# Two cross-attention layers on one core: row-bias sums and weight totals computed in another way, with new orders of the steps

## The chip, the cores and the metric

The kernel runs on one core of a Trainium2 chip. The core has five engines that work at the same time, each strictly in the order of its own instruction stream: TensorE (PE; its weight loads are listed as PEld), VectorE (DVE), ScalarE (ACT), GpSimd (POOL) and SyncE (SP), which here only starts DMAs. They wait for each other through semaphores. SBUF and PSUM are the on-chip memories of 128 partitions; TensorE writes to PSUM. The metric is the device time in microseconds of one execution.

## The reference

For each of 8 batches, `x` is 512 x 256 and `ctx` is 1601 x 128. The first layer's softmax runs over the queries (axis 1), the second's over the context rows. `bq0` and so on are the layer's biases.

```
q = x @ Wq0 + bq0 ; k = ctx @ Wk0 + bk0 ; v = ctx @ Wv0 + bv0
w = softmax(q @ k.T / 16, over the 512 queries)
y = x + w @ v
y = (y - mean) * rsqrt(var + 1e-6) * gamma + beta          # over the 256 features
Q = y @ Wq1 + bq1 ; K = ctx @ Wk1 + bk1 ; V = ctx @ Wv1 + bv1
P = softmax(Q @ K.T / 16, over the 1601 context rows)
out = y + (P @ V) @ Wo + bo
```

## The kernel before

The key projections are folded into the queries: with `A0 = Wq0 @ Wk0.T` the scores of layer 0 are `ctx @ (x A0 + ...).T` plus a term per query, `x @ u0` with `u0 = Wq0 @ bk0`. That term, 512 numbers per batch, is the row bias of layer 0 (`z0`, then `cb`). Layer 1 has the same, `c1`, from the normalised rows `xhat` and `u1_gamma`. As the softmax of layer 0 is over the queries, the weights of one query don't sum to one over the context rows. The value bias `bv0` is therefore multiplied by each query's total weight (`wsum`, then `rowsum0`).

Products that need full precision are made of rounded parts: each operand is split into a high part (ScalarE casts it to float32r) and a low part (the difference, by VectorE where the source is PSUM, by GpSimd where it is SBUF), and `split3` (lines 652 to 656) issues three matmuls.

A batch's 1601 context rows are 13 tiles, 12 of 128 and one of 65. Steps are small functions, named below with (batch, index):

- Layer 0: `turn_ctx` and `turn_x` transpose the inputs on TensorE, `project_q0` makes the folded queries, `project_bias0` spreads `z0` over the partitions, `scores0` makes one tile of scores, `max0` (L1171, VectorE) reads it from PSUM, adds the row bias and takes the extreme, `exp0`, `recip0` and `norm0` make the weights, `p0_high` and `p0_low` (L1383, GpSimd) split them, and `weigh0` accumulates the weighted context. `sum_weights` (L1373, L1376, GpSimd) adds the weights over the tiles into `wsum`, and `sum_rows0` (L748, TensorE) sums that over the partitions, by a matmul with a column of ones.
- Between the layers: `bias_x0` (L1198, L1209, VectorE) adds `rowsum0 * bv0` and `x`, `predict` and `residual0` add the values, `moments0`, `rsqrt_var` (GpSimd) and `normalised` (L1240) give `xhat`, `turn_y` (L768) transposes it and `project_q1` (L774) projects it. `q1_high` (ScalarE) and `q1_low` (L1250, VectorE) split the result.
- Layer 1: `scores1` makes the scores of one block of 128 rows in four chunks, `rowmax1` (L1257) and `bias1_of` (L1268) take the row's maximum and combine it with `c1`, `exp1` (L1048, ScalarE) makes the weights, `turn_p1` (L800) transposes them, `p1_turned` and `p1_low` split them, `weigh1` accumulates, `project_out`, `residual1` (GpSimd) and `finish` (L1290) make the output.

The row biases are made in two steps each. `weigh_u0` (L1407) and `weigh_u1` (L1414) multiply 128 x 1024 elements on GpSimd into the buffer `xr`; `sum_z0` (L1161) and `bias_row1` (L1246) sum them over 256 features on VectorE. `row_bias1` (L1031) then adds a constant on ScalarE. Batch 0's product of layer 0 is made on VectorE (`weigh_u0_first`). A product-and-sum in one instruction exists once, at L1346, for the constant.

Batches are pipelined: while layer 0 works on batch a, layer 1 works on batch b = a - 1, and the first steps of batch c = a + 1 begin. The order of the steps on each engine is written out in tables, one for TensorE, ScalarE, VectorE and GpSimd: a head, a part that is repeated for a = 2 to 5, and a tail. An engine never goes around a step that waits. Loads and stores are issued by SP in a fixed order of their own: the four context groups of a batch, its x, then the store of the batch three before. Each load waits until its buffer is free; the load of x waits for `bias_x0` of the batch two before.

## Time and profile before

| | us |
|---|---|
| median of 3 runs | 467.65 |
| lowest, highest | 466.14, 468.08 |
| profiled execution, first to last instruction (span) | 464.6 |
| TensorE busy | 443.7 (96%) |
| ScalarE busy | 383.7 (83%) |
| VectorE busy | 366.8 (79%) |
| GpSimd busy | 365.0 (79%) |

The profile gives the profiled execution's time as its span alone; the median of the runs lies 3.05 us above it. All times in rows are of that execution, counted from its first instruction. A row's duration reaches from an instruction's start to its end, and the next one on the same engine may start before that end; the distance from start to start is called pitch here. The granted clock of TensorE is 1.00 throughout. TensorE's matmuls overlap a good deal (a 512-column one lasts 0.39 us at a pitch of 0.23), so its cost is read from pitches. In the rows `a<-b,c` is the output and its inputs, `x4` a count, and what stands in square brackets is idle time before the instruction and who ended it.

### The profile page before, as it was taken

Reading aid. Unit: us, or ns where it says so; the run is one execution under the profiler, and the core shown is the slowest. Engines: PE = TensorE matmul, PEld = TensorE weight load, DVE = VectorE, ACT = ScalarE, POOL = GpSimd, SP = SyncE. Lnnn points to the kernel's source line nnn. Section 1 sums busy time; section 2 is a strip of 40 time slices with the busy share of each in tenths; the row PEclk is TensorE's granted clock in tenths of the full one; section 3 lists DMA queues with packets and bytes.
Section 4 is the critical chain, followed back from the end, with each engine's and each line's share of the span. In section 5 each row is a group of like instructions: output and inputs, shape, how many; then the busy total and the mean of one; then the engine's idle time right before and its main releaser. Section 6 shows DMA issues by size and latency. Waiting matters only on the chain.

```text
span 464.6 us, 7967 instructions
## 1 busy us (share of the span) xinstructions
PE 443.7 (96%) x2433; PEld 371.6 (80%) x2433; DVE 366.8 (79%) x898; ACT 383.7 (83%) x819; POOL 365.0 (79%) x321
## 2 busy tenths in 40 slices
PE   8798899999999999999999999999999999799796
PEld 8686667887888888888888878888888878687596
DVE  3798978788886988778787888779877887578774
ACT  4899889987999789987899879987899879872473
...
DMA packets 23896, 17.29 MB, mean 37 GB/s; under 512 B 1055, under 2 KB 23854, under 8 KB 23854
## 3 DMA queue, kind: packets, MB, share of 16 engines
...
## 4 chain that ended last, share of the span: by engine, by line
PE 79%; ACT 8%; DVE 5%; POOL 4%; issue 4%; DVEq 0%; POOLq 0%; ACTq 0%
PE ps_l L654 11%; PE ps_l L655 10%; PE ps_l L656 9%; PE ps_s L800 9%; PE ps_s L654 8%; PE ps_s L656 8%; PE ps_s L655 8%; ACT p L1048 3%; PE ps_s L774 3%; PE ps_s L841 3%; DVE max L1257 2%; POOL wsum L1376 2%; PE ps_l L687 2%; ACT p L1001 2%; PE ps_s L768 2%
## 5 line engine op out<-in xcount | busy, mean ns | idle before, releaser
L1376 POOL TENSOR_TENSOR wsum<-wsum,p 128x512 f32<-128x512 f32 (+1 forms) x88 | 116.3, 1322 | 13.4 <-ACT p L1007 11.8
L1383 POOL TENSOR_TENSOR p_lo<-p,p_hi 128x512 fp32r<-128x512 f32 (+1 forms) x91 | 117.2, 1295 | 2.6 <-ACT p_hi L1015 2.4
L1001 ACT ACTIVATE p<-s_sb,min 128x512 f32<-128x512 f32 (+1 forms) x104 | 75.4, 726 | 7.5 <-DVE min L1171 5.3
L1171 DVE CUSTOM_DVE_ANT_0 s_sb<-ps_l,cb 128x512 f32<-128x512 f32 (+1 forms) x104 | 70.4, 685 | 13.3 <-ACT p L1001 5.5
L1007 ACT ACTIVATE p<-p,r 128x512 f32<-128x512 f32 (+1 forms) x104 | 74.9, 728 | 1.4 <-DVE r L1178 1.3
L1192 DVE TENSOR_TENSOR p1T_lo<-ps_s,p1T_hi 128x512 fp32r<-128x512 f32 (+1 forms) x91 | 60.6, 683 | 14.4 <-ACT p1T_hi L1056 13.9
L1257 DVE TENSOR_REDUCE max<-ps_s 128x1 f32<-128x804 f32 x58 | 57.1, 992 | 10.0 <-PE ps_s L656 8.6
L1056 ACT CAST p1T_hi<-ps_s 128x512 fp32r<-128x512 f32 (+1 forms) x91 | 52.0, 586 | 14.9 <-PE ps_s L800 12.1
L1015 ACT CAST p_hi<-p 128x512 fp32r<-128x512 f32 (+1 forms) x104 | 63.5, 624 | 0.5 <-PE ps_l L656 0.4
L1048 ACT ACTIVATE p<-ps_s,bias 128x1206 f32<-128x1206 f32 (+1 forms) x58 | 53.6, 927 | 3.6 <-DVE bias L1268 3.1
L800 PE MATMUL ps_s<-ident,p 128*128 128x128 f32 (+1 forms) x364 | 49.6, 273 | 1.5 <-ACT p L1048 1.5
L800 PEld LDWEIGHTS ps_s<-ident,p 128*128 128x128 f32 (+1 forms) x364 | 43.2, 141 | 9.3 <-ACT p L1048 1.9
L654 PE MATMUL ps_l<-p_hi,ctx_lo 128*128 128x512 f32 (+1 forms) x104 | 45.5, 437 | 2.4 <-POOL p_lo L1383 2.2
L654 PE MATMUL ps_l<-qw_hi,ctxT_lo 128*128 128x512 f32 (+1 forms) x104 | 46.6, 448 | 0.7 <-DVE min L1171 0.7
L1364 POOL TENSOR_TENSOR ctx_lo<-ctx_sb,ctx_hi 128x512 fp32r<-128x512 f32 (+1 forms) x32 | 35.2, 1101 | 12.4 <-ACT ctx_hi L974 12.4
L654 PE MATMUL ps_s<-p1T_hi,ctx_lo 128*128 128x512 f32 (+2 forms) x104 | 43.9, 422 | 0.8 <-DVE p1T_lo L1280 0.8
L654 PE MATMUL ps_s<-ctxT_hi,qw_lo 128*128 128x402 f32 x116 | 42.2, 364 | 2.2 <-ACT p L1048 2.0
L656 PE MATMUL ps_l<-p_hi,ctx_hi 128*128 128x512 f32 (+1 forms) x104 | 41.0, 394 | 0.0
L655 PE MATMUL ps_l<-qw_lo,ctxT_hi 128*128 128x512 f32 (+1 forms) x104 | 41.0, 394 | 0.0
L656 PE MATMUL ps_l<-qw_hi,ctxT_hi 128*128 128x512 f32 (+1 forms) x104 | 41.0, 394 | 0.0
L655 PE MATMUL ps_l<-p_lo,ctx_hi 128*128 128x512 f32 (+1 forms) x104 | 40.9, 393 | 0.0
L656 PE MATMUL ps_s<-ctxT_hi,qw_hi 128*128 128x402 f32 x116 | 40.0, 345 | 0.0
...
## 6 DMA issues: line engine op xcount, KB each, us to landing
...
```

Source lines behind the costliest of these rows:

```text
L654: nc.tensor.matmul(ps, w_lo, m_hi, start=start, stop=False)
L655: nc.tensor.matmul(ps, w_hi, m_lo, start=False, stop=False)
L656: return nc.tensor.matmul(ps, w_hi, m_hi, start=False, stop=stop)
L800: mm = nc.tensor.transpose(ps_turn[i % 3][0:m, t * P:(t + 1) * P], p1[:, t, i * P:i * P + m], ident[:])
L1001: nc.scalar.activation(p0[0:m, ring0(i), :], s0_sb[0:m, (a + i) % 2, :], ACT.Exp, bias=min0[0:m, i:i + 1], scale=-1.0, accum_out=sum0[0:m, ...
L1007: nc.scalar.activation(p0[0:m, ring0(i), :], p0[0:m, ring0(i), :], ACT.Copy, scale=r0[0:m, i:i + 1]).then_inc(norm0_done, 1)
L1015: nc.scalar.copy(p0_hi[0:m, (MT * a + i) % RH, :], p0[0:m, ring0(i), :]).then_inc(p0_hi_done, 1)
L1048: nc.scalar.activation(exps, scores, ACT.Exp, bias=bias1[:, t:t + 1], scale=1.0, accum_out=sum1[:, h, t:t + 1]).then_inc(exp1_done, 1)
L1171: nc.vector.tensor_tensor_reduce(out=s0_sb[0:m, (a + i) % 2, :], in0=ps_s0[0:m, (a + i) % 2, :], in1=cb[a % 2][0:m, :], scale=-SCALE, scal ...
L1257: nc.vector.tensor_reduce(max1[:, t, k:k + 1], s1_banks(b, t)[:, 2 * k:2 * k + 2, 0:CHUNK], AX_XY, ALU.max).then_inc(max1_done, 1)
L1376: nc.gpsimd.tensor_tensor(total, total, p0[0:m, ring0(i), :], ALU.add).then_inc(wsum_done, 1)
L1383: nc.gpsimd.tensor_tensor(p0_lo[0:m, h, :], p0[0:m, ring0(i), :], p0_hi[0:m, h, :].bitcast(F32), ALU.subtract).then_inc(p0_lo_done, 1)
```

## The change

- `weigh_u0_first`, `weigh_u0`, `sum_z0` and `weigh_u1` are removed. `row_bias0` and the new `bias_row1` make each row bias with four product-and-sum instructions of 128 x 256 on VectorE; their product goes to `xr` and is not used, and layer 1's constant comes in as the start value of the sum. `row_bias1` on ScalarE is removed.
- `sum_rows0` transposes the four blocks of `wsum` into the whole PSUM bank, and `bias_x0` sums over 128 columns each on VectorE.
- The waits are adapted: a group now counts four. `row_bias0` of batch a waits for `bias_row1` of batch a - 2, since both write `xr`; `bias_x0` waits for both as before.
- All four order tables are new. The last part of an iteration now holds layer 1's first steps and `turn_x`, `x_turned` and `xT_low` of batch a + 2 (role "d").

The code parts of the diff, and of the order tables the new repeated parts of VectorE and GpSimd, the end of TensorE's and the beginning of ScalarE's:

```
 TENSOR_STEADY = (
...
+    ("weigh1", "b", 6), ("weigh1", "b", 7), ("turn_p1", "b", 11), ("predict", "a", 0), ("weigh1", "b", 8),
+    ("weigh1", "b", 9), ("predict", "a", 1), ("turn_p1", "b", 12), ("scores0", "c", 5), ("weigh1", "b", 10),
+    ("weigh1", "b", 11), ("weigh1", "b", 12), ("turn_ctx", "c", 2), ("weigh0", "c", 0), ("project_out", "b", 0),
+    ("project_out", "b", 1), ("turn_y", "a", 0), ("turn_y", "a", 1), ("turn_x", "d", 0), ("scores0", "c", 6),
+    ("project_q1", "a", 0), ("weigh0", "c", 1), ("weigh0", "c", 2), ("scores0", "c", 7),
...
 SCALAR_STEADY = (
...
+    ("norm0", "a", 6), ("exp0", "a", 7), ("exp1", "b", 0), ("x_turned", "c", 1), ("norm0", "a", 7), ("exp1", "b", 1),
+    ("exp0", "a", 8), ("p0_high", "a", 6), ("norm0", "a", 8), ("p0_high", "a", 7), ("exp1", "b", 2),
+    ("q0_high", "c", 0), ("exp1", "b", 3), ("exp0", "a", 9), ("p0_high", "a", 8), ("ctx_high", "a", 3),
+    ("norm0", "a", 9), ("exp0", "a", 10), ("exp1", "b", 4), ("p0_high", "a", 9), ("exp1", "b", 5), ("norm0", "a", 10),
...
 VECTOR_STEADY = (
-    ("bias_row1", "b", 0), ("q1_low", "b", 0), ("recip0", "a", 5), ("max0", "a", 6), ("max0", "a", 7),
...
-    ("rowmax1", "b", 3), ("bias1_of", "b", 1), ("max0", "a", 9), ("max0", "a", 10), ("sum_z0", "c", 0),
+    ("recip0", "a", 7), ("max0", "a", 8), ("max0", "a", 9), ("xT_low", "c", 1), ("rowmax1", "b", 2),
+    ("recip0", "a", 8), ("rowmax1", "b", 3), ("bias1_of", "b", 1), ("row_bias0", "c", 0), ("max0", "a", 10),
     ("q0_low", "c", 0), ("rowmax1", "b", 4), ("recip0", "a", 9), ("rowmax1", "b", 5), ("bias1_of", "b", 2),
...
-    ("recip0", "c", 3), ("p1_low", "b", 12), ("residual0", "a", 1), ("moments0", "a", 1), ("normalised", "a", 0),
-    ("normalised", "a", 1), ("max0", "c", 4), ("ctxT_low", "c", 2), ("recip0", "c", 4), ("finish", "b", 0),
-    ("finish", "b", 1), ("max0", "c", 5),
+    ("ctxT_low", "a", 3), ("max0", "a", 11), ("recip0", "a", 10), ("max0", "a", 12), ("rowmax1", "b", 6),
+    ("rowmax1", "b", 7), ("bias1_of", "b", 3), ("ctxT_low", "c", 0), ("recip0", "a", 11), ("max0", "c", 0),
+    ("max0", "c", 1), ("recip0", "a", 12), ("p1_low", "b", 0), ("p1_low", "b", 1), ("recip0", "c", 0),
+    ("p1_low", "b", 2), ("p1_low", "b", 3), ("p1_low", "b", 4), ("max0", "c", 2), ("ctxT_low", "c", 1),
+    ("recip0", "c", 1), ("max0", "c", 3), ("p1_low", "b", 5), ("p1_low", "b", 6), ("p1_low", "b", 7),
+    ("bias_x0", "a", 0), ("recip0", "c", 2), ("p1_low", "b", 8), ("at0_low", "a", 0), ("p1_low", "b", 9),
+    ("p1_low", "b", 10), ("recip1", "b", 0), ("recip0", "c", 3), ("residual0", "a", 0), ("moments0", "a", 0),
+    ("residual0", "a", 1), ("p1_low", "b", 11), ("p1_low", "b", 12), ("moments0", "a", 1), ("normalised", "a", 0),
+    ("max0", "c", 4), ("normalised", "a", 1), ("ctxT_low", "c", 2), ("bias_row1", "a", 0), ("recip0", "c", 4),
+    ("finish", "b", 0), ("finish", "b", 1), ("max0", "c", 5), ("xT_low", "d", 0), ("max0", "c", 6),
+    ("q1_low", "a", 0), ("recip0", "c", 5), ("max0", "c", 7), ("rowmax1", "a", 0), ("recip0", "c", 6),
+    ("rowmax1", "a", 1), ("bias1_of", "a", 0),
 )
...
 GPSIMD_STEADY = (
-    ("rsqrt_var", "b", 0), ("p0_low", "a", 1), ("sum_weights", "a", 2), ("rsqrt_var", "b", 1), ("weigh_u1", "b", 0),
...
-    ("weigh_u0", "c", 0), ("p0_low", "a", 6), ("sum_weights", "a", 7), ("p0_low", "a", 7), ("sum_weights", "a", 8),
...
+    ("p0_low", "a", 3), ("p0_low", "a", 4), ("sum_weights", "a", 4), ("ctx_low", "a", 2), ("p0_low", "a", 5),
+    ("sum_weights", "a", 5), ("sum_weights", "a", 6), ("p0_low", "a", 6), ("p0_low", "a", 7), ("sum_weights", "a", 7),
+    ("p0_low", "a", 8), ("sum_weights", "a", 8), ("sum_weights", "a", 9), ("p0_low", "a", 9), ("p0_low", "a", 10),
+    ("residual1", "b", 0), ("sum_weights", "a", 10), ("sum_weights", "a", 11), ("sum_weights", "a", 12),
+    ("p0_low", "a", 11), ("p0_low", "a", 12), ("ctx_low", "a", 3), ("sum_weights", "c", 1), ("p0_low", "c", 0),
+    ("p0_low", "c", 1), ("rsqrt_var", "a", 0), ("ctx_low", "c", 0), ("p0_low", "c", 2), ("rsqrt_var", "a", 1),
+    ("ctx_low", "c", 1), ("sum_weights", "c", 2), ("sum_weights", "c", 3),
 )
...
@@ -710,7 +699,7 @@
                 mm.then_inc(qw0_ps, 1)
 
             def project_bias0(a, _):
-                pe.wait_ge(z0_done, a + 1)
+                pe.wait_ge(z0_done, TB * (a + 1))
                 misc_free("project_bias0", a)
                 for t in range(TB):
                     mm = nc.tensor.transpose(ps_misc[:, t * P:(t + 1) * P], z0[:, t:t + 1].broadcast_to([P, P]), ident[:])
@@ -745,8 +734,7 @@
                 pe.wait_ge(wsum_done, summed(a, MT - 1))
                 misc_free("sum_rows0", a)
                 for t in range(TB):
-                    mm = nc.tensor.matmul(ps_misc[:, t:t + 1], wsum[a % 2][:, t * P:(t + 1) * P], ones[:, 0:1],
-                                          start=True, stop=True)
+                    mm = nc.tensor.transpose(ps_misc[:, t * P:(t + 1) * P], wsum[a % 2][:, t * P:(t + 1) * P], ident[:])
                 mm.then_inc(rowsum_ps, 1)
 
             def predict(a, h):
@@ -1026,10 +1014,6 @@
                     act.wait_ge(row1_made, MADE)
                 nc.scalar.copy(xhT[:, c, :], ps_y[c]).then_inc(xhT_done, 1)
 
-            def row_bias1(b, _):
-                act.wait_ge(c1_part_done, b + 1)
-                nc.scalar.activation(c1[:], c1_part[:], ACT.Identity, bias=c1_const[:, 0:1], scale=1.0).then_inc(c1_done, 1)
-
             def q1_high(b, _):
                 act.wait_ge(qw1_ps, b + 1)
@@ -1147,18 +1131,18 @@
                 nc.vector.scalar_tensor_tensor(qw0_lo[a % 2][:], ps_misc[:], qb0, qw0_hi[a % 2][:].bitcast(F32),
                                                ALU.add, ALU.subtract).then_inc(qw0_lo_done, 1)
 
-            def weigh_u0_first(a, _):
-
-                dve.wait_ge(u0_done, 1)
-                dve.wait_ge(x_loaded[0], 16)
-                nc.vector.tensor_tensor(xr[:], x_sb[0][:], u0_row[:].unsqueeze(1).broadcast_to([P, TB, E]), ALU.mult
-                                        ).then_inc(xu0_done, 1)
-
-            def sum_z0(a, _):
-                dve.wait_ge(xu0_done, a + 1)
+            def row_bias0(a, _):
+
+                if a == 0:
+                    dve.wait_ge(u0_done, 1)
+                if a >= 2:
+                    dve.wait_ge(c1_done, TB * (a - 1))
                 if a > 0:
                     dve.wait_ge(cb_ps, a)
-                nc.vector.tensor_reduce(z0[:], xr[:], AX_X, ALU.add).then_inc(z0_done, 1)
+                dve.wait_ge(x_loaded[a % 2], 16 * (a // 2 + 1))
+                for t in range(TB):
+                    nc.vector.tensor_tensor_reduce(out=xr[:, t, :], in0=x_sb[a % 2][:, t, :], in1=u0_row[:], scale=1.0, scalar=0.0,
+                                                   op0=ALU.mult, op1=ALU.add, accum_out=z0[:, t:t + 1]).then_inc(z0_done, 1)
 
             def max0(a, i):
 
@@ -1195,14 +1179,15 @@
             def bias_x0(a, _):
 
                 dve.wait_ge(rowsum_ps, a + 1)
-                nc.vector.tensor_copy(rowsum0[:], ps_misc[:, 0:TB]).then_inc(rowsum_done, 1)
+                nc.vector.tensor_reduce(rowsum0[:], ps_misc[:].rearrange("p (t m) -> p t m", m=P), AX_X, ALU.add
+                                        ).then_inc(rowsum_done, 1)
                 if a == 0:
                     dve.wait_ge(rows_loaded, 16 * 2)
                     dve.wait_ge(row1_made, MADE)
                 else:
-                    dve.wait_ge(c1_part_done, a)
+                    dve.wait_ge(c1_done, TB * a)
                 if a < B - 1:
-                    dve.wait_ge(z0_done, a + 2)
+                    dve.wait_ge(z0_done, TB * (a + 2))
                 dve.wait_ge(x_loaded[a % 2], 16 * (a // 2 + 1))
                 dve.wait_ge(rowsum_done, a + 1)
                 for t in range(TB):
@@ -1242,8 +1227,15 @@
 
             def bias_row1(b, _):
 
-                dve.wait_ge(u1_part_done, b + 1)
-                nc.vector.tensor_reduce(c1_part[:], xr[:], AX_X, ALU.add).then_inc(c1_part_done, 1)
+                dve.wait_ge(xhat_done, TB * (b + 1))
+                if b == 0:
+                    dve.wait_ge(row1_made, MADE)
+                else:
+                    dve.wait_ge(bias1_done, TB * b)
+                for t in range(TB):
+                    nc.vector.tensor_tensor_reduce(out=xr[:, t, :], in0=xhat[:, t, :], in1=u1_gamma[:], scale=1.0,
+                                                   scalar=c1_const[:, 0:1], op0=ALU.mult, op1=ALU.add,
+                                                   accum_out=c1[:, t:t + 1]).then_inc(c1_done, 1)
 
             def q1_low(b, _):
                 dve.wait_ge(qw1_hi_done, b + 1)
@@ -1260,7 +1252,7 @@
             def bias1_of(b, t):
 
                 if t == 0:
-                    dve.wait_ge(c1_done, b + 1)
@@ -1397,23 +1389,6 @@
                     ins = nc.gpsimd.tensor_tensor(y_res[:, t, :], y_res[:, t, :], betaob_row[:], ALU.add)
                 ins.then_inc(y_res_done, 1)
 
-            def weigh_u0(a, _):
-
-                pool.wait_ge(x_loaded[a % 2], 16 * (a // 2 + 1))
-                if a == 1:
-                    pool.wait_ge(z0_done, a)
-                else:
-                    pool.wait_ge(c1_part_done, a - 1)
-                nc.gpsimd.tensor_tensor(xr[:], x_sb[a % 2][:], u0_row[:].unsqueeze(1).broadcast_to([P, TB, E]), ALU.mult
-                                        ).then_inc(xu0_done, 1)
-
-            def weigh_u1(b, _):
-
-                pool.wait_ge(xhat_done, TB * (b + 1))
-                pool.wait_ge(row1_made, MADE)
-                nc.gpsimd.tensor_tensor(xr[:], xhat[:], u1_gamma[:].unsqueeze(1).broadcast_to([P, TB, E]), ALU.mult
-                                        ).then_inc(u1_part_done, 1)
-
             def rsqrt_var(a, h):
                 pool.wait_ge(var_done, 2 * a + h + 1)
                 two = slice(2 * h, 2 * h + 2)
```

## Rows read from the trace of the kernel before

**Rows 1.** The page's part 1: busy time, share and instructions of each engine.

```profile
PE 443.7 (96%) x2433; PEld 371.6 (80%) x2433; DVE 366.8 (79%) x898; ACT 383.7 (83%) x819; POOL 365.0 (79%) x321
```

**Rows 2.** Three stretches: us; busy of PE, PEld, DVE, ACT, POOL; clock, DMA.

```profile
50.00:102.00 52.00, 49.15 (x260) 39.42 (x259) 41.93 (x104) 47.26 (x100) 47.83 (x42) 1.00 0.09 28
208.30:261.50 53.20, 52.95 (x289) 44.59 (x288) 43.55 (x107) 46.79 (x100) 47.50 (x42) 1.00 0.12 36
370.00:418.60 48.60, 45.45 (x243) 37.55 (x241) 35.28 (x88) 38.79 (x80) 42.34 (x38) 1.00 0.03 11
```

**Rows 3.** The chain that ended last: start, length in us, what.

```profile
285.22 1.81 DVE max L1257 x2
287.56 1.37 ACT p L1048 x2
```

**Rows 4.** TensorE in order of time: start, length in us; two places.

```profile
202.98 0.95 PE L748 MATMUL ps_l<-ones,wsum 128*128 128x1 f32 x8
203.79 0.47 PE L654 MATMUL ps_l<-p_hi,ctx_lo 128*128 128x512 f32 x1
...
239.90 0.60 PE L716 MATMUL ps_l<-ident,z 128*128 128x128 f32 x4
240.25 0.48 PE L654 MATMUL ps_l<-qw_hi,ctxT_lo 128*65 128x512 f32 x1
```

**Rows 5.** By form: line, engine, op, count; busy us, mean ns; idle before.

```profile
L1414 POOL TENSOR_TENSOR xr<-xhat,u_gamma 128x1024 f32<-128x1024 f32 x8 | 19.0, 2380 | 5.1 <-DVE xhat L1240 5.1
...
L1280 DVE TENSOR_TENSOR p1T_lo<-ps_s,p1T_hi 128x256 fp32r<-128x256 f32 x24 | 9.3, 420 | 4.8 <-ACT p1T_hi L1063 4.0
```

**Rows 6.** VectorE in order of time, around the row sum of layer 0.

```profile
233.87 0.68 DVE L1171 CUSTOM_DVE_ANT_0 s_sb<-ps_l,cb 128x512 f32<-128x512 f32 x1
234.47 0.69 DVE L1171 CUSTOM_DVE_ANT_0 s_sb<-ps_l,cb 128x512 f32<-128x512 f32 x1
235.08 1.21 DVE L1161 TENSOR_REDUCE z<-xr 128x4 f32<-128x1024 f32 x1
236.21 0.74 DVE L1147 SCALAR_TENSOR_TENSOR qw_lo<-ps_l,small,qw_hi 128x512 fp32r<-128x512 f32 x1
```

**Rows 7.** A wait of an operation with two SBUF inputs: VectorE, then GpSimd.

```profile
98.57 0.88 DVE L1209 SCALAR_TENSOR_TENSOR xr<-bv_row,rowsum,x_sb 128x256 f32<-128x256 f32 x1
...
97.86 1.30 POOL L1383 TENSOR_TENSOR p_lo<-p,p_hi 65x512 fp32r<-65x512 f32 x1
```

**Rows 8.** The product-and-sum that is already there: VectorE, then GpSimd.

```profile
38.28 0.79 DVE L1346 CUSTOM_DVE_ANT_0 xhat<-p,scaled 128x256 f32<-128x256 f32 x1
...
36.96 1.82 POOL L1376 TENSOR_TENSOR wsum<-wsum,p 128x512 f32<-128x512 f32 x1
```

**Rows 9.** The operation of rows 7 with GpSimd idle: VectorE.

```profile
258.28 1.67 DVE L1209 SCALAR_TENSOR_TENSOR xr<-bv_row,rowsum,x_sb 128x256 f32<-128x256 f32 x4
```

**Rows 10.** Around the normalised rows: VectorE, then GpSimd, then TensorE.

```profile
216.01 0.73 DVE L1240 TENSOR_SCALAR xhat<-xr,mv,rstd 128x256 f32<-128x256 f32 x2 [0.27 <-POOL rstd L1420]
218.84 1.66 DVE L1290 SCALAR_TENSOR_TENSOR y_res<-ps_s,r,y_res 128x256 f32<-128x256 f32 x4
222.88 0.75 DVE L1250 SCALAR_TENSOR_TENSOR qw_lo<-ps_s,scaled,qw_hi 128x512 fp32r<-128x512 f32 x1 [0.47 <-ACT qw_hi L1035]
...
224.16 3.90 POOL L1383 TENSOR_TENSOR p_lo<-p,p_hi 128x512 fp32r<-128x512 f32 x3
...
217.97 1.04 PE L768 MATMUL ps_s<-ident,xhat 128*128 128x128 f32 x8
220.24 1.88 PE L774 MATMUL ps_s<-xhT,a_gamma 128*128 128x512 f32 x4
224.03 0.35 PE L654 MATMUL ps_s<-ctxT_hi,qw_lo 128*128 128x402 f32 x1
```

**Rows 11.** The place in layer 1's scores: ScalarE, then TensorE.

```profile
239.43 1.27 ACT L1048 ACTIVATE p<-ps_s,bias 128x1206 f32<-128x1206 f32 x1
...
241.03 0.34 PE L654 MATMUL ps_s<-ctxT_hi,qw_lo 128*128 128x402 f32 x1
```

More of the change, by code:

```diff
@@ L287 @@
[L287 removed]
[3 rows of a table removed]
[L291 to L293 removed]
+    ("sum_weights", 0, 11), ("sum_weights", 0, 12), ("sum_weights", 1, 1), ("ctx_low", 1, 0), ("p0_low", 1, 0),
@@ new lines @@
+    ("sum_weights", 6, 11), ("sum_weights", 6, 12), ("p0_low", 6, 11), ("p0_low", 6, 12), ("ctx_low", 6, 3),
+    ("residual1", 5, 0), ("sum_weights", 7, 1), ("p0_low", 7, 0), ("ctx_low", 7, 0), ("rsqrt_var", 6, 0),
+    ("rsqrt_var", 6, 1), ("p0_low", 7, 1), ("p0_low", 7, 2), ("sum_weights", 7, 2), ("p0_low", 7, 3),
+    ("p0_low", 7, 4), ("ctx_low", 7, 1), ("sum_weights", 7, 3), ("sum_weights", 7, 4), ("p0_low", 7, 5),
+    ("sum_weights", 7, 5), ("p0_low", 7, 6), ("p0_low", 7, 7), ("sum_weights", 7, 6), ("sum_weights", 7, 7),
@@ L319 @@
+    ("sum_weights", 7, 8), ("p0_low", 7, 8), ("sum_weights", 7, 9), ("ctx_low", 7, 2), ("p0_low", 7, 9),
+    ("p0_low", 7, 10), ("p0_low", 7, 11), ("sum_weights", 7, 10), ("sum_weights", 7, 11), ("sum_weights", 7, 12),
+    ("p0_low", 7, 12), ("ctx_low", 7, 3), ("residual1", 6, 0), ("rsqrt_var", 7, 0), ("rsqrt_var", 7, 1),
+    ("residual1", 7, 0),
 )
@@ L1350, in _ @@
             steps = {f.__name__: f for f in (
-                ctxT_low, xT_low, at0_low, bias_x0, q0_low, weigh_u0_first, sum_z0, max0, recip0, residual0, moments0, normalised, bias_row1,
+                ctxT_low, xT_low, at0_low, bias_x0, q0_low, row_bias0, max0, recip0, residual0, moments0, normalised, bias_row1,
                 q1_low, rowmax1, bias1_of, recip1, p0_low_first, p1_low, p1_low_half, finish, prepare_w1)}
@@ L1429, in _ @@
             steps = {f.__name__: f for f in (
-                ctx_low, sum_weights, p0_low, rsqrt_var, weigh_u0, weigh_u1, residual1)}
+                ctx_low, sum_weights, p0_low, rsqrt_var, residual1)}
             pre0()
```

58 lines of the change are left out of this document (25 added, 33 removed), and 433 rows, old and new, of tables (GPSIMD_HEAD, GPSIMD_STEADY, SCALAR_HEAD, SCALAR_STEADY).

## The prediction

> **What bounds the kernel now.** I read the shares first [rows 1], then the stages, then the chain of waits, then single places in order of time. The shares say TensorE: 443.7 of 464.6 us, the other three near 80%. The stages say where [rows 2]: in a middle batch (53.20 us long) TensorE is busy 52.95, VectorE 43.55, GpSimd 47.50. It is idle for 2.85 us in the second batch's stretch and for 3.15 in the seventh's; only there does a slack GpSimd have something to give. So in the middle only two things count: TensorE instructions saved, and anything that comes so late that TensorE waits. The second is near, though TensorE looks full: the chain leaves it in every middle batch for two maxima of layer 1's scores on VectorE and two exponentials on ScalarE before TensorE goes on [rows 3]. VectorE has 9.65 us idle per batch, but it works in order, and a delay in front of such a maximum is not spread over them.
>
> **The change part by part.**
>
> *sum_rows0.* Four fp32 matmuls with one column are eight instructions and hold TensorE from 202.98 to 203.79, 0.81 us. Four transposes of 128x128, here those of z, take 239.90 to 240.25, 0.35 us [rows 4]. The saving is 0.46 us per batch, 8 x 0.46 = 3.7 us, all of it on the path in the middle.
>
> *bias_x0.* The copy of 4 columns becomes a sum over 512 columns in PSUM: some 0.6 us by the pitch of a 512-wide operation [rows 6], instead of under 0.1, so 0.5 us more VectorE per batch. It lies beside weigh0 and weigh1 on TensorE; sum_rows0 also moves ahead of the last weigh0 steps. Cost 0; without that cover it would be 0.5 x 8 = 4 us.
>
> *GpSimd's products go.* 2.38 us each [rows 5], two per batch, 4.8 of 47.5 us, so GpSimd falls to 42.7 of 53.2, 80%. In the middle GpSimd is not the bound, so this is worth 0 there. At the two ends it may shorten the waits for p_lo and wsum. The ends are 0 and the whole idle time of the two stretches, 6.0 us [rows 2]. I take half, 3.0. ScalarE's row_bias1 (four columns) goes too: 0.
>
> *VectorE's product-and-sums.* Each group of four replaces one reduction of 1024 columns, which is 1.13 us of VectorE (235.08 to 236.21). Alone, a product-and-sum over 512 columns has a pitch of 0.60 with its accumulator read (233.87 to 234.47) [rows 6]. 256 columns less are 0.27 less (0.69 us for 512 columns [rows 6] against 420 ns for 256 [rows 5]). So one costs 0.33 and a group 1.33, 0.2 us more than now. That is nothing, if nothing else happens.
>
> But these operations read both inputs from SBUF, unlike the maxima in layer 0, whose first input is PSUM. The trace shows what happens to such a one while GpSimd is at work. bias_x0's operation started at 98.57, GpSimd's running one ended at 99.16, and it ended at 99.45 [rows 7]: 0.29 after GpSimd's end, instead of 0.48 after its own start. The product-and-sum that exists already started at 38.28 and ended at 39.07, GpSimd's at 38.78, again 0.29 later [rows 8]. So it waits until GpSimd's whole instruction is over, then needs its own time. With GpSimd idle four such operations take 1.67 us [rows 9]; seven of the eight groups of bias_x0 are like that, because GpSimd happens to be waiting there. The new groups stand elsewhere.
>
> The Trainium skill, "SBUF — State Buffer", section "Who interferes with whom", says that a VectorE instruction with two SBUF inputs and a GpSimd instruction that reads SBUF shut each other out, and that the one issued second waits for the first one's end. The traces agree where they show it (0.29 after GpSimd's end, twice). By that rule a waiting GpSimd instruction also gets in between two of a group's four, which would give the forecast below; without it the sum would be the first rival's.
>
> The waits per group: the first operation meets a running GpSimd instruction four times in five (80% load), on average half over. One lasts 1.25 us by pitch (three in 3.90) [rows 10]: 0.5 us. For the other three no row shows who gets in when VectorE's one ends with GpSimd waiting. The ends are 0 (VectorE keeps its turn) and 3 x 1.25 + 1.25 = 5.0 in all. I take turns one after the other where GpSimd has work ready, since the rows show that neither breaks into the other.
>
> *Site 1, bias_row1.* It stands behind normalised and ctxT_low, ahead of finish, max0, xT_low, max0 and q1_low. GpSimd then has ctx_low, two sum_weights and a p0_low in line, all but the last fed early by ScalarE; with such a line it runs without a gap today [rows 10]. Wait W1 = 0.5 + two more of 1.25 = 3.0. How much is hidden? xhat is done at 216.66 (216.01 and two pitches of 0.33). Then 0.60 + 1.33 + 0.10 + 1.73 + 0.61 + 0.61 + 0.61 brings VectorE to q1_low at 222.25. qw_hi, now there at 222.88, comes 0.37 earlier, since turn_y is followed by a turn of x and one scores0 only (1.90 instead of the 2.27 from 217.97 to 220.24): 222.51. q1_low ends at 223.20; TensorE reaches scores1 at 223.7 (224.03 less 0.37) [rows 10]. Slack 0.26 + 0.50 = 0.76; TensorE waits 3.0 - 0.76 = 2.2 us.
>
> *Site 2, row_bias0.* It stands behind bias1_of of the second row block, ahead of max0, q0_low and the next two maxima, which feed the exponential before the last scores1. Today that exponential ends at 240.70 and scores1 starts at 241.03: slack 0.33 [rows 11]. One max0 (0.61) now comes before the site instead of behind, against 0.2 for the group: slack 0.7. GpSimd has p0_low and sum_weights of tile 7 ready, then waits for p0_high of tile 8, which ScalarE issues behind two exponentials. W2 = 0.5 + 1.25 + 0.8 x 1.25 = 2.7; TensorE waits 2.0 us.
>
> Both sites recur in 6 batches with layer 0 and layer 1 side by side: 6 x 4.2 = 25 us. In the first two and the last batch I add nothing, since TensorE is idle there anyway; its cover gone it would be some 2 us each.
>
> *The orders anew.* The same steps with neighbours exchanged; turn_x of the batch after next now comes an iteration early, and its x is loaded by then, as the x load is released by bias_x0 of the batch whose buffer it takes. SP's and GpSimd's queues keep the loads' order. I give this 0, bounds -4 and +6: the waits of the middle batches today are 0.25 us each by [rows 2], so there is little to win there.
>
> The sum against the profiled execution, span 464.6: -3.7 - 3.0 + 25.2 = +18.5, 483.1. The median of the runs is 467.65, 3.05 above the span, so 486.
>
> **The rivals.** *Hidden: the change simply works.* GpSimd, with 4.8 us less to do, has often nothing ready when a group comes, or VectorE keeps its turn after one wait of 0.5, which is under both slacks (0.76 and 0.7). Then 464.6 - 3.7 - 3.0 = 457.9, or 461 as a run; from 457 with all of the 6.0 us to 464 with none of it. For it speaks the eight bias_x0 groups, seven of them untouched [rows 9]; against it that GpSimd's idle time there came from a wait for ctx_hi, which the new sites do not share. It decides in its favour if the waits per group stay under 0.7 us.
>
> *A wash.* The first wait is a whole instruction each time, 1.25: 0.5 us at site 1 and 0.6 at site 2, 6.6 us in six batches, against 6.7 saved: 464.5, 467.6 as a run.
>
> *VectorE becomes the bound.* All four of a group wait for 1.25: W = 5.0, waits of 4.2 and 4.3 us, 51 us in six batches: 464.6 - 3.7 + 51 = 512, 515 as a run. VectorE's 43.6 + 0.9 + 10 us would then exceed today's period. Against it: GpSimd would have to be never short of work, while each TensorE wait starves it.
>
> **How the numbers follow.** Forecast (group waits of 1.6 to 4 us, so 471 to 500): 0.52. Works: 0.33. A wash: 0.10. VectorE the bound: 0.05. This kernel's runs tell about 0.5% from no change, 2.3 us. Faster is the first rival, 0.33; same 0.10; slower 0.57. The range is 457 to 506; the forecast's own is 471 to 500. The bounds of the orders (-4, +6) are in it.
>
> **What would show it.** Right: in the middle batches the product-and-sums of 256 columns have means well over 0.42 us, 0.9 to 1.3, with ends some 0.29 behind the end of a GpSimd instruction; GpSimd's instructions beside them are up to 0.3 longer; TensorE's busy share falls to some 92%, with waits for qw_lo and for the exponentials in front of scores1; a middle batch takes 57 us. The transposes of wsum take 0.35 us per batch, the sum over 512 columns 0.6. Wrong: mean product-and-sums at 0.42 us, TensorE at 96% or more and a middle batch at or under 52.8 us. The forecast fails above all if VectorE's four go through in a row with GpSimd waiting behind them, or if GpSimd is idle at both sites.

## The result, and the profile after

The changed kernel takes 520.24 us (median of 4 runs, 519.62 to 520.71) against 467.38 for the kernel before on the same chip: ratio 1.1138, 95% interval 1.1117 to 1.1158. It is slower, as forecast, but by 53 us instead of 18, and outside the range. One of the five executions of all_gated_first below took 2482.68 us; it is left out of that kernel's median and ratio.

The page's part 1 of the kernel after, to be held against [rows 1]:

```profile
PE 459.9 (89%) x2401; PEld 374.5 (72%) x2401; DVE 426.6 (82%) x1009; ACT 385.6 (74%) x811; POOL 337.7 (65%) x306
```

A middle batch takes 62.0 us, against 53.3 before, by the starts of bias_x0 (204.97 and 258.28 before). The stretch of one such batch (columns as in [rows 2]), and a piece of it:

```profile
246.10:308.10 62.00, 55.55 (x286) 45.26 (x285) 52.61 (x121) 47.17 (x100) 43.95 (x39) 0.97 0.10 31
256.60:259.90 3.30, 3.30 (x12) 3.27 (x11) 1.27 (x4) 2.12 (x6) 3.29 (x4) 0.50 0.01 2
```

GpSimd did get 3.6 us lighter than in [rows 2] and nobody gained from it; VectorE is busy for 9.1 us more. TensorE is idle for 6.45 us of the batch instead of 0.25. The three groups of four on VectorE, each line with min/median/max ns, the first start and the last:

```profile
L1236 DVE CUSTOM_DVE_ANT_0 xr<-xhat,u_gamma,c_const x32: 473/1302/1510, 68.9 to 484.6; 128x256 f32<-128x256 f32 x32
L1144 DVE CUSTOM_DVE_ANT_0 xr<-x_sb,u_row x32: 413/552/1547, 12.2 to 392.6; 128x256 f32<-128x256 f32 x32
L1194 DVE SCALAR_TENSOR_TENSOR xr<-bv_row,rowsum,x_sb x32: 477/867/1530, 55.7 to 468.9; 128x256 f32<-128x256 f32 x32
```

Site 1 (bias_row1, L1236) in one batch, VectorE and GpSimd merged in order of time:

```profile
246.18 1.28 POOL L1356 TENSOR_TENSOR ctx_lo<-ctx_sb,ctx_hi 128x512 fp32r<-128x512 f32 x1 [1.29 <-ACT ctx_hi L962]
246.44 1.30 DVE L1236 CUSTOM_DVE_ANT_0 xr<-xhat,u_gamma,c_const 128x256 f32<-128x256 f32 x1
247.42 2.88 POOL L1368 TENSOR_TENSOR wsum<-wsum,p 128x512 f32<-128x512 f32 x2
247.68 1.50 DVE L1236 CUSTOM_DVE_ANT_0 xr<-xhat,u_gamma,c_const 128x256 f32<-128x256 f32 x1
249.11 1.48 DVE L1236 CUSTOM_DVE_ANT_0 xr<-xhat,u_gamma,c_const 128x256 f32<-128x256 f32 x1
250.26 1.48 POOL L1375 TENSOR_TENSOR p_lo<-p,p_hi 128x512 fp32r<-128x512 f32 x1
250.51 1.51 DVE L1236 CUSTOM_DVE_ANT_0 xr<-xhat,u_gamma,c_const 128x256 f32<-128x256 f32 x1
```

The first waits for ctx_lo (over at 247.46) and ends 0.28 later; then the two engines take turns, one whole instruction each, so that the second to fourth take 1.5 us where their own time is 0.48. An operation that waits like this is called caught below. The group takes 5.6 us. What TensorE does behind it:

```profile
254.33 0.50 PE L643 MATMUL ps_l<-qw_hi,ctxT_lo 128*128 128x512 f32 x1 [2.61 <-DVE min L1155]
256.29 0.46 PE L643 MATMUL ps_s<-ctxT_hi,qw_lo 128*128 128x402 f32 x1 [1.00 <-DVE qw_lo L1242]
257.21 0.54 PE L643 MATMUL ps_s<-ctxT_hi,qw_lo 128*128 128x402 f32 x1
270.16 0.34 PE L644 MATMUL ps_s<-ctxT_lo,qw_hi 128*128 128x402 f32 x1
```

It waits 2.61 us for a max0 that stands behind the group, then 1.00 for q1_low. After that its granted clock is 0.50, the lower of its two levels, for about 3.4 us; matmuls of 402 columns start 0.33 apart instead of 0.18, which costs 1.5 us more. Each of the four batches whose bias_row1 is caught three times or more (183.9 to 370.4 us) has such a stretch behind it (6.8 us long in the first of them); the batch from 121.1 to 183.6, whose bias_row1 is caught once, has none (granted clock 1.00), and before no middle batch had one.

Site 2 (267.24 to 270.99) has two operations of 1.5 us. The third group is bias_x0's, which is no new operation. Its four took 1.67 us in [rows 9] and take 3.74 here; TensorE waits 1.42 us behind them:

```profile
293.54 0.68 DVE L1182 TENSOR_REDUCE rowsum<-ps_l 128x4 f32<-128x512 f32 x1
294.36 3.74 DVE L1194 SCALAR_TENSOR_TENSOR xr<-bv_row,rowsum,x_sb 128x256 f32<-128x256 f32 x4
295.05 1.35 POOL L1365 TENSOR_TENSOR wsum<-p 128x512 f32<-128x512 f32 x1 [1.83 <-ACT p L995]
296.35 1.47 POOL L1375 TENSOR_TENSOR p_lo<-p,p_hi 128x512 fp32r<-128x512 f32 x1
298.82 0.66 PE L788 MATMUL ps_s<-ident,p 128*128 128x128 f32 x4 [1.42 <-DVE p1T_lo L1176]
```

### The profile page after: what moved, and what is told of

It is laid out like the page before. It is cut to its first block, busy times and chain, and to the rows that moved or that the text cites. A ratio compares the mean times of both kernels' runs of the same rounds, so it can differ in the third digit from the quotient of the medians.

```text
span 518.1 us, 7984 instructions
## 1 busy us (share of the span) xinstructions
PE 459.9 (89%) x2401; PEld 374.5 (72%) x2401; DVE 426.6 (82%) x1009; ACT 385.6 (74%) x811; POOL 337.7 (65%) x306
## 4 chain that ended last, share of the span: by engine, by line
DVE 36%; PE 25%; POOL 18%; issue 15%; ACT 5%; DVEq 0%; POOLq 0%; ACTq 0%
POOL wsum L1368 6%; POOL p_lo L1375 5%; DVE p1T_lo L1176 5%; DVE xr L1194 4%; PE ps_l L643 4%; DVE xr L1144 4%; PE ps_l L644 4%; PE ps_l L645 4%; DVE s_sb L1155 3%; DVE xr L1236 3%; PE ps_s L643 3%; DVE max L1249 2%; POOL y_res L1385 2%; POOL y_res L1389 2%; PE ps_s L644 2%
## 5 line engine op out<-in xcount | busy, mean ns | idle before, releaser
L1375 POOL TENSOR_TENSOR p_lo<-p,p_hi 128x512 fp32r<-128x512 f32 (+1 forms) x91 | 118.8, 1313 | 52.1 <-ACT p_hi L1003 51.9
L1176 DVE TENSOR_TENSOR p1T_lo<-ps_s,p1T_hi 128x512 fp32r<-128x512 f32 (+1 forms) x91 | 59.3, 683 | 12.8 <-ACT p1T_hi L1040 12.4
L1003 ACT CAST p_hi<-p 128x512 fp32r<-128x512 f32 (+1 forms) x104 | 62.4, 617 | 1.8 <-PE ps_l L645 1.3
L1040 ACT CAST p1T_hi<-ps_s 128x512 fp32r<-128x512 f32 (+1 forms) x91 | 50.6, 586 | 15.6 <-PE ps_s L788 14.2
L643 PE MATMUL ps_s<-ctxT_hi,qw_lo 128*128 128x402 f32 x116 | 45.7, 394 | 7.3 <-DVE qw_lo L1242 4.4
L643 PE MATMUL ps_l<-p_hi,ctx_lo 128*128 128x512 f32 (+1 forms) x104 | 46.7, 449 | 1.0 <-POOL p_lo L1375 0.9
L644 PE MATMUL ps_s<-ctxT_lo,qw_hi 128*128 128x402 f32 x116 | 42.5, 367 | 0.0
L643 PE MATMUL ps_s<-p1T_hi,ctx_lo 128*128 128x512 f32 (+2 forms) x104 | 42.2, 406 | 0.4 <-DVE p1T_lo L1176 0.4
L645 PE MATMUL ps_s<-ctxT_hi,qw_hi 128*128 128x402 f32 x116 | 42.4, 365 | 0.0
```

What stands on the lines that cost most here:

```text
L643: nc.tensor.matmul(ps, w_lo, m_hi, start=start, stop=False)
L644: nc.tensor.matmul(ps, w_hi, m_lo, start=False, stop=False)
L645: return nc.tensor.matmul(ps, w_hi, m_hi, start=False, stop=stop)
L1003: nc.scalar.copy(p0_hi[0:m, (MT * a + i) % RH, :], p0[0:m, ring0(i), :]).then_inc(p0_hi_done, 1)
L1176: nc.vector.tensor_tensor(p1T_lo[0:m, i % RING, :], ps_turn[i % 3][0:m, :], p1T_hi[0:m, i % RING, :].bitcast(F32), ALU.subtract).then_inc( ...
L1375: nc.gpsimd.tensor_tensor(p0_lo[0:m, h, :], p0[0:m, ring0(i), :], p0_hi[0:m, h, :].bitcast(F32), ALU.subtract).then_inc(p0_lo_done, 1)
```

## The experiments

All ratios are to the kernel before, with their 95% intervals; "after" is 520.2 us.

### Is it the second input?

**one_input_row1, one_input_row0, one_input_both**: the product-and-sums at one or both sites become row sums of one input (u0 and u1 drop out).

```
-  nc.vector.tensor_tensor_reduce(out=xr[:, t, :], in0=xhat[:, t, :], in1=u1_gamma[:], ..., accum_out=c1[:, t:t + 1])
+  nc.vector.tensor_reduce(c1[:, t:t + 1], xhat[:, t, :], AX_X, ALU.add)     # row0: z0 and x_sb in the same way
```

> Only bias_row1's four read one SBUF input (its product is left out). Theory: its place is worth 3.9 us of TensorE waits and most of the 1.5 us at half clock per middle batch, so 485 to 492. If the wait at bias_x0 and row_bias0 grows in its place, 500 or more.

> Only row_bias0's four read one SBUF input (its product is left out). Theory: 1.3 to 2 us per middle batch and up to 4 us in the first batch, where TensorE waits for z: 505 to 511.

> The changed kernel, but each of the 2 x 4 product-and-sums per batch is a plain sum of one SBUF input of 256 columns (the multiplication by u0 and u1_gamma and the constant are left out). Orders, waits, instruction count and VectorE's own time stay (0.35 to 0.42 us each). Theory (the two-input operations wait for GpSimd's instructions): each takes 0.42 us, the middle batch loses the TensorE waits of 2.8 and 1.2 us at bias_row1 and 1.3 us at row_bias0 and most of the half clock, about 7 of 62 us; time 475 to 482, with bias_x0's wait left. Rival (the new orders, or VectorE's longer work, are too tight by themselves): the time stays at 505 to 520.

Measured: 496.0 (1.0627, 1.0573 to 1.068), 506.9 (1.086, 1.0824 to 1.0895) and 481.2 (1.0309, 1.0271 to 1.0346). The 32 sums of site 2 in the last one, on the same place between the same GpSimd instructions:

```profile
L1144 DVE TENSOR_REDUCE z<-x_sb x32: 408/410/415, 12.2 to 353.2; 128x1 f32<-128x256 f32 x32
```

None waited. Site 1 alone is worth 24.2 us (the time is 4 us over its range; the other two are in theirs), site 2 13.3, both 39.1, about their sum. But 14 us over before remain.

A sum of one input differs from a product-and-sum in its output too: one column instead of 256. That the output is not the cause shows in the kernel after itself, where max0 has one input in PSUM and one in SBUF, writes 512 columns to SBUF and is never caught:

```profile
L1155 DVE CUSTOM_DVE_ANT_0 s_sb<-ps_l,cb x104: 664/681/693, 20.2 to 456.8; 128x512 f32<-128x512 f32 x96, 65x512 f32<-65x512 f32 x8
```

**one_input_all**: bias_x0 as well is given an operation with one SBUF input (bv0 drops out).

```
-  nc.vector.scalar_tensor_tensor(xr[:, t, :], bv0_row[:], rowsum0[:, t:t + 1], x_sb[a % 2][:, t, :], ALU.mult, ALU.add)
+  nc.vector.tensor_scalar(xr[:, t, :], x_sb[a % 2][:, t, :], rowsum0[:, t:t + 1], rowsum0[:, t:t + 1], ALU.subtract, ALU.mult)
```

> As one_input_both, and bias_x0's four operations too read one SBUF input (they leave out the value bias). Theory: a third place of the same wait goes, 2.1 us of VectorE and 1.8 us of TensorE per middle batch, so 10 to 13 us less than one_input_both, 461 to 469 in all, at or under the kernel before. Rival (orders too tight): within 3 us of one_input_both.

Measured: 478.3 (1.0246, 1.0208 to 1.0284), a miss. It lies within the rival's 3 us of one_input_both, which says nothing for the rival, since the experiment did not take away what it meant to:

```profile
266.81 3.43 DVE L1193 TENSOR_SCALAR xr<-x_sb,rowsum 128x256 f32<-128x256 f32 x4
267.49 1.30 POOL L1362 TENSOR_TENSOR wsum<-p 128x512 f32<-128x512 f32 x1 [1.83 <-ACT p L995]
268.75 1.34 POOL L1372 TENSOR_TENSOR p_lo<-p,p_hi 128x512 fp32r<-128x512 f32 x1
```

A tensor_scalar from SBUF to SBUF takes 0.41 us alone and 1.38 to 1.48 beside GpSimd, though it has one SBUF input. The Trainium skill, "SBUF — State Buffer", section "Who interferes with whom", has both halves of it: it says that tensor_scalar can enter a mode that takes both port pairs, and that tensor_reduce on trn2 never contends. The rows agree as to which of the two is caught. That the tensor_scalar was in such a mode they do not show: alone it takes 0.41 us, as long as the tensor_reduce.

**one_product**: one product over 1024 columns and one reduction per group instead of four product-and-sums.

```
-  for t in range(TB): tensor_tensor_reduce(... xr[:, t, :] ..., accum_out=z0[:, t:t + 1])
+  nc.vector.tensor_tensor(xr[:], x_sb[a % 2][:], u0_row[:] repeated TB times, ALU.mult)
+  nc.vector.tensor_reduce(z0[:], xr[:], AX_X, ALU.add)                      # bias_row1 likewise, plus its constant
```

> The changed kernel with each group of four product-and-sums replaced by one product of 128 x 1024 and one sum on VectorE: 2.3 us of own work instead of 1.4, but one wait for GpSimd instead of up to four. Theory (one wait of at most 1.27 per two-input instruction): bias_row1's place shrinks from 5.5 to about 3.5 us, row_bias0's from 3.6 to about 3.2; 500 to 508. Rival (VectorE's amount of work is the matter): 525 or more, as 1.8 us per batch are added.

Measured: 506.5 (1.0842, 1.0808 to 1.0875), in the theory's range, 14 us less than after. There are fewer turns, but a product and a sum take 2.4 us by themselves (1.22 each) against 1.5 or 1.7 for the four, and layer 1's constant is now an operation of its own, a tensor_scalar of four columns, which is caught as well (0.23 us at the least, 0.96 in the median, 1.23 at the most).

**before_sums**: the kernel before with the product-and-sums where the old sums stood, old orders, one-column products kept.

```
+  row_bias0 and bias_row1 of the kernel after, at the places of sum_z0 and bias_row1
-  ("weigh_u0", ...), ("weigh_u1", ...), ("row_bias1", ...) in the three orders
```

> The kernel before with the other part alone: product-and-sums on VectorE in place of GpSimd's products, at the places of the old orders; row totals and orders as before. Theory (waits for GpSimd): 1.2 to 1.5 us for most of the eight per batch, 500 to 520. Rival (the new orders cost it): at most 472. With new orders half to blame: 485 to 495.

Measured: 519.4 (1.1118, 1.1083 to 1.1152), as slow as the whole change. The product-and-sums are enough; the new orders are not needed for it. The two times are made up differently, though: here bias_x0 is hardly caught (0.75 us at the most instead of 0.48), and in the middle batches the other two groups take 4.7 and 5.2 us.

### The transposes

**before_transposes**: only the transposes and the sum over 512 columns.

```
-  nc.tensor.matmul(ps_misc[:, t:t + 1], wsum[a % 2][:, t * P:(t + 1) * P], ones[:, 0:1], start=True, stop=True)
+  nc.tensor.transpose(ps_misc[:, t * P:(t + 1) * P], wsum[a % 2][:, t * P:(t + 1) * P], ident[:])
-  nc.vector.tensor_copy(rowsum0[:], ps_misc[:, 0:TB])
+  nc.vector.tensor_reduce(rowsum0[:], ps_misc[:].rearrange("p (t m) -> p t m", m=P), AX_X, ALU.add)
```

> The kernel before with one part of the change alone: sum_rows0 by four transposes and bias_x0's sum over 512 columns. Old orders, products on GpSimd. The forecast's term: 0.46 us of TensorE saved per batch, 3.7 us in all, VectorE's 0.5 us per batch hidden: 463 to 465. Rival (the longer sum on VectorE delays a maximum): no gain, 467 or more.

Measured: 486.2 (1.0409, 1.0392 to 1.0426), a clear miss: the part priced at -3.7 costs 19 us, all of it in the four batches (2 to 5) where bias_x0 is caught (from its start in batch 2 to that in batch 6 it is 232.2 us, and 213.1 before). Its bias_x0 in one batch, and who waits:

```profile
212.51 4.80 DVE L1209 SCALAR_TENSOR_TENSOR xr<-bv_row,rowsum,x_sb 128x256 f32<-128x256 f32 x4
212.92 1.29 POOL L1364 TENSOR_TENSOR ctx_lo<-ctx_sb,ctx_hi 128x512 fp32r<-128x512 f32 x1 [1.32 <-ACT ctx_hi L973]
214.16 1.46 POOL L1373 TENSOR_TENSOR wsum<-p 128x512 f32<-128x512 f32 x1
215.59 1.44 POOL L1383 TENSOR_TENSOR p_lo<-p,p_hi 128x512 fp32r<-128x512 f32 x1
218.06 0.36 PE L654 MATMUL ps_l<-wv_hi,at_lo 128*128 128x256 f32 x1 [3.17 <-DVE at_lo L1136]
219.48 0.63 PE L656 MATMUL ps_s<-p1T_hi,ctx_hi 128*128 128x512 f32 x1
```

In the kernel before, the fourth of [rows 9] starts at 259.48 and GpSimd's ctx_low at 259.70, 0.22 us too late to get in. Here ctx_low starts together with the second, three are caught, at_low is late, TensorE waits 3.17 us and then works at the lower clock (0.63 us for 0.39).

**before_long_sum**: the one-column products kept, only the read changed to the sum over 512 columns.

> The kernel before, its one-column products by the ones column kept, only the read of them replaced by the sum over all 512 columns of the bank (the values of the other columns are left over from earlier work, so that the row sums are not the reference's). It has the 0.5 us longer sum and not the transposes. Theory (the 0.5 us alone shift bias_x0 into GpSimd's operations): 484 to 490 us, as before_transposes or up to 3.7 above it. Rival (it is the transposes that cost): 467 to 471.

Measured: 473.8 (1.0143, 1.013 to 1.0156), between what theory and rival gave. bias_x0 in one batch:

```profile
154.55 2.70 DVE L1210 SCALAR_TENSOR_TENSOR xr<-bv_row,rowsum,x_sb 128x256 f32<-128x256 f32 x4
155.44 1.53 POOL L1365 TENSOR_TENSOR ctx_lo<-ctx_sb,ctx_hi 128x512 fp32r<-128x512 f32 x1 [1.83 <-ACT ctx_hi L974]
```

In before_transposes the same batch has bias_x0 at 154.53 and ctx_low at 154.94. So the longer sum makes the group late by 0.5 us, and the transposes, which save TensorE 0.46 us, bring ScalarE's ctx_hi and with it GpSimd's ctx_low 0.5 us earlier. The longer sum alone catches the last operation, the two together catch three. A saving on one engine costs here because it brings another engine's instruction into the group.

**transposes_gated**: before_transposes, with one wait on GpSimd.

```
 def ctx_low(a, g):
+    if g == 0 and a > 0:
+        pool.wait_ge(xbias_done, a)
```

> The kernel before with the transposes and the 512-column sum, and one wait more: GpSimd's low part of the next batch's first context group (ctx_low(c, 0)) starts only when bias_x0's four operations are through. Theory (the 486.2 of before_transposes come from bias_x0's last three operations being caught between GpSimd's at 212.92, 214.16 and 215.59): with the wait they last 0.48 us each again, ctx_low starts about 0.8 us later and nothing waits for it, so 463 to 466 us (467.4 less eight times the 0.46 us that the transposes are shorter than the one-column products). Rival (the longer sum or the transposes are themselves what costs): 480 to 487. Rival 2 (GpSimd's work is late by the wait and TensorE waits for it): 470 to 478.

Measured: 467.65 against 467.01, 12 and 17 runs (1.0017, 1.0006 to 1.0028).

```profile
L1209 DVE SCALAR_TENSOR_TENSOR xr<-bv_row,rowsum,x_sb x32: 476/477/485, 50.0 to 417.7; 128x256 f32<-128x256 f32 x32
```

One wait gives back the 19 us but for 0.6; the time is 1.7 over the theory's range. The 3.7 us of the transposes do not appear. In a middle batch two short waits of TensorE stand in their place:

```profile
258.88 0.19 PEld L654 LDWEIGHTS ps_l<-p_hi,ctx_lo 65*128 65x128 f32 x1 [0.16 <-POOL p_lo L1385]
...
208.02 0.69 DVE L1136 TENSOR_TENSOR at_lo<-ps_l,at_hi 128x512 fp32r<-128x512 f32 x1
208.42 0.39 PE L656 MATMUL ps_s<-p1T_hi,ctx_hi 128*128 128x512 f32 x1
208.85 0.36 PE L654 MATMUL ps_l<-wv_hi,at_lo 128*128 128x256 f32 x1
```

The earlier TensorE comes to the last tile before GpSimd's p_low is ready (in the kernel before it came 0.35 us after), and at_low, which stands behind the longer sum, holds it up by 0.2 us (a start 0.43 us after the one before instead of 0.23). That is 0.37 of the 0.46 us.

### All three groups without the turns

**one_input_gated**: one_input_both with a wait for bias_x0 on GpSimd.

```
 def sum_weights(a, i):
+    if i == 1 and a > 0:
+        pool.wait_ge(xbias_done, a)
```

> As one_input_both (row sums of one input at both new places, which leaves out the products with u0 and u1), with one wait more on GpSimd: the first sum of the next batch's weights (sum_weights(c, 1)) starts only when bias_x0 is through. Theory (of the 14 us that one_input_both is over before, most is the third place, bias_x0's four operations at 3.7 instead of 1.7 us and what follows from them): 464 to 471 us. Rival (the rest is the new orders themselves): 476 to 482, as without the wait.

Measured: 472.1 (1.0116, 1.0099 to 1.0133), 9.1 us under one_input_both and 1 over the expected range. The third group is worth 9.1 us. A middle batch (210.12 to 262.68) takes 52.6 us, so in the middle the new orders are no worse than the old ones.

5.1 us over before remain, and the trace shows a fourth group behind them: normalised, a tensor_scalar with one SBUF input. Its second pair is caught in batches 0, 1 and 6 (1.35 us each instead of 0.41), here and in the kernel after; before, none was. The first line is of this kernel, the second of the kernel before, in which no matmul waits for xhat. The third has turn_y's waits in this kernel (us in all, times, the longest):

```profile
L1224 DVE TENSOR_SCALAR xhat<-xr,mv,rstd x32: 399/406/1351, 58.5 to 432.4; 128x256 f32<-128x256 f32 x32
L1240 DVE TENSOR_SCALAR xhat<-xr,mv,rstd x32: 400/408/415, 56.8 to 425.8; 128x256 f32<-128x256 f32 x32
PE ps_s L756 <- DVE xhat L1224: 5.2, 3, 2.0
```

These waits are as large as the rest. No run takes them away, so that they are what is left is read from the trace and not shown.

**all_gated**: the kernel after, whole, with that wait and two more.

```
 def ctx_low(a, g):
+    if g == 1 and a > 0:
+        pool.wait_ge(c1_done, TB * a)
 def p0_low(a, i):
+    if i == 7 and a < B - 1:
+        pool.wait_ge(z0_done, TB * (a + 2))
```

> The kernel after, whole, with three waits more on GpSimd and nothing else: ctx_low(c, 1) starts after bias_row1's four product-and-sums, sum_weights(c, 1) after bias_x0's four, and p0_low(a, 7) after row_bias0's four. All that the change computes on VectorE stays there. Theory (what costs is the taking of turns with GpSimd, 5.5, 3.65 and 3.7 us per batch instead of 1.7 each, not VectorE's added work): 464 to 476 us, the upper part if p0_low(a, 7), up to 1.4 us later, holds TensorE up. Rival 1 (VectorE has become too full by the 3.3 us added per batch): 485 to 500. Rival 2 (the waits move the loss to GpSimd's late split parts): 495 to 520.

Measured: 479.8 (1.0268, 1.0255 to 1.0281): 40.4 of the 53 us are gone though VectorE does everything it did in the kernel after; 4 us over the upper end of the theory, 5 under the nearest rival. Some turns remain: row_bias0 of batch 0 is caught three times, that of batch 2 twice. One batch and its site 1:

```profile
217.80:270.50 52.70, 52.51 (x287) 44.06 (x285) 44.92 (x121) 47.06 (x99) 42.96 (x39) 1.00 0.12 37
```

```profile
L1236 DVE CUSTOM_DVE_ANT_0 xr<-xhat,u_gamma,c_const x32: 471/476/488, 67.0 to 444.6; 128x256 f32<-128x256 f32 x32
...
who waited for it (us, times):
  POOL ctx_lo L1358: 19.3, 6
```

GpSimd stands idle 3.2 us per batch for it (19.3 in six) and TensorE does not notice: the batch is 0.6 us shorter than before's, VectorE's busy time falls from 52.6 to 44.9 us. What is left is lost ahead of bias_x0 of batch 2, which starts at 165.1 us, before's at 151.8.

**all_gated_first**: row_bias0(0) ahead of ctxT_low(0, 0), and ctx_low(0, 0) waits for it.

> all_gated (479.8 us) with two edits at the start: row_bias0(0) stands ahead of ctxT_low(0, 0), and ctx_low(0, 0) on GpSimd waits until its four operations are through. In all_gated TensorE waits 4.2 us for them at 12 us and then works at half clock for a stretch. Theory (this place is worth 5 to 6 of the 12 us): 474 to 476. Rival (the four context splits that now start 1 us later are late for the weighted sums instead): 478 to 481.

Measured: 475.2 (1.0177, 1.0156 to 1.0198), in the theory's range: the first batch's group, caught three times while TensorE waited 4.0 us for z, is worth 4.5 us. 8.1 remain. TensorE's three waits for normalised (5.2 us in all) are in this kernel too, and row_bias0 of batch 2 is still caught twice.

**old_orders_gated, old_orders_gated_copy**: before_sums with bias_row1 moved up to normalised(b, 1), and GpSimd waits for all three groups; with transposes, and without them.

```
+  def after_row1(b, _): pool.wait_ge(c1_done, TB * (b + 1))     # where weigh_u1 stood
+  def after_row0(a, _): pool.wait_ge(z0_done, TB * (a + 1))     # ahead of p0_low(a - 1, 7)
+  ctx_low(a, 0) with a > 0 waits for xbias_done
```

> The whole change on VectorE and TensorE (product-and-sums at both places, transposes and the 512-column sum) in the orders of the kernel before, with bias_row1 placed two or three steps behind normalised(b, 1), and GpSimd waiting at three places until VectorE's four operations are through: where weigh_u1 stood, ahead of p0_low(a, 7), and ahead of ctx_low(c, 0). Theory (the change itself costs nothing once the operations don't take turns, and the 12 us by which all_gated is still over before come from the new orders of the first two batches: its bias_x0 of batch 1 starts at 108.3 instead of 98.6, and its middle batches take 52.7 us against 53.3): 461 to 467 us. Rival (the 12 us belong to the product-and-sums in VectorE's queue, in whatever order): 474 to 482.

> As old_orders_gated, but with the one-column products and the four-column copy of the kernel before instead of the transposes and the long sum. By the matmul starts the transposes give 0.46 us per batch, which transposes_gated did not show in its time (467.65). Theory (they are worth it where TensorE waits for nothing else): 2 to 4 us more than old_orders_gated. Rival (the 0.5 us longer sum at the end of the batch takes it back): equal to old_orders_gated within 1 us.

Measured: 473.3 (1.0144, 1.0122 to 1.0166) and 471.8 (1.0115, 1.0098 to 1.0132). Both expectations missed: the first is 6 us over its range and just under its rival's, and the copy is faster by 1.5 instead of slower by 2 to 4. So transposes and longer sum together give nothing in this kernel even with the turns gone. The middle batches are those of before (53.4 to 53.7); in the first, bias_x0 of batch 1 starts 5.5 us late.

**old_orders_head**: in the first, two waits placed better.

```
+  ("after_row0", 1, 0) ahead of ("sum_weights", 0, 3)
-  ("after_row0", 2, 0) ahead of ("p0_low", 1, 7)
+  ("after_row0", 2, 0) ahead of ("sum_weights", 1, 7)
```

> old_orders_gated (473.3 us) with its GpSimd waits of the first two batches put better: one ahead of sum_weights(0, 3), so that row_bias0(1), which at 26.4 us was caught twice (1.48 and 1.49 us instead of 0.42), runs alone, and the one for row_bias0(2) ahead of sum_weights(1, 7) instead of p0_low(1, 7) (two operations caught at 78 us). Theory (the 5.5 us that its first two batches lie behind before, bias_x0 of batch 1 at 104.1 against 98.6, are these two groups and the stretch of half clock at 29 to 33 us that the first brings): 467 to 470. Rival (they come from bias_row1(0)'s and the sums' length in a VectorE that is full there): 472 to 475.

Measured: 470.03 (1.0062, 1.0045 to 1.0078), at the upper end of the theory's range. This is the fastest version that computes everything in the new way (its orders are the old ones), and it is still 2.9 us slower than the kernel before. No version beat that one.

## Why the prediction was wrong

**Right.** The direction, the bound (TensorE, with waits that late VectorE results end), and the mechanism: operations with two SBUF inputs and GpSimd's instructions shut each other out and take turns. The choice between the ends of W was for strict turns, and the traces show nothing else. What the cited section of the Trainium skill says of two SBUF inputs held in every group. Alone, four product-and-sums take 1.5 us at site 2 and 1.7 at site 1 (priced 1.33). GpSimd's relief brought nothing in the middle.

**Right by luck.** Site 2 was priced at 2.0 us times 6, 12 us, and measured at 13.3. But of these 13.3, 7.0 lie ahead of bias_x0 of batch 1 (111.2 us in the kernel after, 104.2 in one_input_row0), where the forecast added nothing; the next five batches add 6.0, 1.2 each (413.1 and 400.1 us at bias_x0 of batch 6). Only with site 1 free is a middle batch 1.9 us longer by it (56.4 us in one_input_row1, 54.5 in one_input_both).

**Wrong, in order of size.** The forecast was 34 us short.

1. *Site 1, 2.2 us in each of six batches, 13 in all; measured 24.2.* Some 22 of these fall on the four batches 2 to 5, about 5.5 each. Two terms failed. W1 was 3.0, which is 0.5 for the first operation and two more of 1.25; the group takes 5.6 us instead of 1.7, so 3.9, which is 0.8 for the first and 1.0 for each of the other three, since all three were caught. And the end was looked for at q1_low only: the max0 behind the group came to TensorE first (2.61 us, then 1.00 for q1_low), and the lower clock that followed (1.5 us per batch) was in no term.
2. *"In the first two and the last batch I add nothing, since TensorE is idle there anyway."* Before, bias_x0 of batch 1 starts at 98.6 us, after at 111.2: 12.6 us lost. In one_input_gated, where the three groups are free up to there, it starts at 101.7, so some 9.5 of the 12.6 are their turns; the first group alone is worth 4.5.
3. *bias_x0, "Cost 0".* The third group was measured at 9.1 us in the new orders, and its longer sum alone at 6.8 in the old ones. The step named TensorE's work as the cover. The real cover stands beside [rows 9]: GpSimd was waiting for ctx_hi. It was read as evidence on the new sites, and not as a gap with 0.2 us to spare that the same change closes.
4. *Transposes, -3.7.* The 0.46 us exist in the starts of the matmuls, and the time never showed them: 467.65 against 467.01 in one pair, 1.5 us worse in the other. The words "all of it on the path" left out p_low and at_low, each ready less than 0.5 us before TensorE needs it.
5. *Orders, 0, and ends, -3.0 for GpSimd's relief.* In the middle the first holds (52.6 us a batch against 53.3), within its bounds. At the ends the new orders let a fourth group be caught, normalised, for which TensorE waits 5.2 to 5.3 us in all; the prediction looked for such waits only at operations with two SBUF inputs. Of the -3.0 nothing was seen, but no run tells it apart from the rest.

Taken together: both sites were priced at 25.2 us and measured at 39.1, bias_x0's group at 0 and measured at 9.1, and 5.1 are left (one_input_gated) where the sum had -6.7 for the savings and 0 for the orders.

The rival *VectorE becomes the bound* gave 515 and came nearest by its number. Half of its mechanism came about: at site 1 all four of a group wait. But they wait 3.9 us and not 5.0, site 2's wait 2.3, and VectorE is not the bound: it is busy 52.6 of the 62.0 us in the kernel after, and at least 7.7 of these 52.6 are waiting that the profile counts as busy, since with most turns gone and the same work it is busy 44.9.
